# SP fetches the sixteenth gather of each step's last tile row by row, from row numbers loaded into registers

## What is computed

```
q = x @ Wq_pk;  sim = q . keys                 # per head, per side: 128 scores a token
scores, idx = top_k(sim, 16)                   # two sides
score = scores0[:, None] + scores1[None, :]    # 16 x 16 sums
final_scores, pk_idx = top_k(score, 16);  final_scores = softmax(final_scores)
ind = index[pk_idx] + head * 16384             # 16 rows of a table a token and head
k = sum_16 final_scores * keys_table[ind];  v = sum_16 final_scores * values_table[ind]
out = softmax(causal(q k^T)) v;  x = x + out @ Wo
```

## Time and profile before

| | |
|---|---|
| median of 3 runs | 10316.75 us (10314.2 to 10340.01) |
| the profiled execution, its own time | 10337.94 us |
| its span | 10336.0 us |
| busy: POOL, PE, DVE, ACT | 7772.2, 4872.7, 4777.3, 1478.0 us |
| granted PE clock, mean | 0.599 of full speed |

### The profile page before, as it was taken

One profiled execution on the slowest core, in us unless ns is written; L12 is line 12 of the kernel. 1 busy time (PEld: TensorE's weight loads), 2 busy tenths in 40 slices (PEclk: granted clock), 3 DMA queues, 4 the chain that ended last, 5 costly groups with the idle time before them and its releaser, 6 DMA issues.

```text
span 10336.0 us, 99229 instructions
## 1 busy us (share of the span) xinstructions
PE 4872.7 (47%) x26912; PEld 2864.2 (28%) x26912; DVE 4777.3 (46%) x21897; ACT 1478.0 (14%) x4051; POOL 7772.2 (75%) x8201
## 2 busy tenths in 40 slices
PE   4444444544445444444444444444444444444444
PEld 2222222322223222232222222222222222322222
DVE  5454444444444444444444444444454444444443
ACT  1111111111111111111111111111111111111111
POOL 6777777777777777777777777777777777777776
PEclk6565655656555565565655656556565565655655
DMA  3333333333333333333333333333333333333333
GB/s 106 105 111 105 105 111 105 111 105 105 111 105 111 105 105 112 105 111 105 105 111 105 112 105 105 111 105 111 105 105 111 105 111 105 105 111 105 106 105 97
DMA packets 420780, 1106.51 MB, mean 107 GB/s; under 512 B 131952, under 2 KB 149744, under 8 KB 420208
## 3 DMA queue, kind: packets, MB, share of 16 engines
q0 software_dynamic: 393216, 1074.27, 36.1%
q1 hardware_dynamic: 27120, 27.46, 0.9%
HBM read 1097.01 MB, written 4.19 MB: 107 GB/s over the span
## 4 chain that ended last, share of the span: by engine, by line
POOL 74%; issue 25%; PE 1%; POOLq 0%; DMA 0%; DVE 0%; ACT 0%; DVEq 0%
POOL got L242 74%; PE comb_ps L347 0%; DMA got<-in_table,rows 0%; POOLq L235 0%; POOLq L238 0%; POOLq L239 0%; POOLq L236 0%; PE front_ps L292 0%; POOLq L249 0%; PE front_ps L281 0%; PE score_ps L368 0%; PE score_ps L380 0%; DVE xn L584 0%; PE front_ps L272 0%; PE front_ps L311 0%
## 5 line engine op out<-in xcount | busy, mean ns | idle before, releaser
L242 POOL DMA_INDIRECT got<-in_table,rows x8192 | 7770.4, 949 | 2538.5 <-issue 2492.1
L347 PE MATMUL comb_ps<-got,spread 128*32 128x256 f32 x16384 | 1564.5, 548 | 3665.8 <-DMA got<-in_table,rows 3665.8
L347 PEld LDWEIGHTS comb_ps<-got,spread 128*32 128x32 f32 x16384 | 637.4, 150 | 4468.2 <-DMA got<-in_table,rows 3788.8
L725 DVE CUSTOM_DVE_ANT_0 neg<-score_ps,mask 128x128 f32<-128x128 f32 (+3 forms) x512 | 251.7, 492 | 2393.0 <-PE score_ps L368 2387.3
L745 DVE SCALAR_TENSOR_TENSOR acc<-probT_ps,prob_inv,acc 128x128 f32<-128x128 f32 x448 | 157.1, 351 | 1628.7 <-PE probT_ps L386 1628.7
L380 PE MATMUL score_ps<-probT,kv 128*128 128x128 f32 x2560 | 691.6, 433 | 269.6 <-ACT probT L426 269.6
L426 ACT ACTIVATE keyT<-probT_ps 128x128 f32<-128x128 f32 x512 | 142.1, 278 | 4198.5 <-PE probT_ps L358 4020.6
L368 PE MATMUL score_ps<-keyT,qT 128*128 128x128 f32 (+3 forms) x1024 | 578.9, 656 | 330.3 <-DVE spread L701 177.4
L374 PE MATMUL probT_ps<-ident,prob 128*128 128x128 f32 x1280 | 356.8, 397 | 754.8 <-ACT prob L502 754.8
L380 PEld LDWEIGHTS score_ps<-probT,kv 128*128 128x128 f32 x2560 | 550.5, 308 | 432.0 <-ACT probT L426 432.0
L374 PEld LDWEIGHTS probT_ps<-ident,prob 128*128 128x128 f32 x1280 | 194.8, 188 | 1138.7 <-ACT prob L502 1138.7
(11 more groups left out here) (99 smaller groups left out, 5640.1 us busy)
## 6 DMA issues: line engine op xcount, KB each, us to landing
got<-in_table,rows POOLq DMA_INDIRECT x8192, 2.7
adj_i<-in_adj SPq DMA_DIRECT2D x16, 1024.0 KB
x_in<-in_x SPq DMA_DIRECT2D x16, 256.0 KB, 3.5
out<-fin SPq DMA_DIRECT2D x16, 256.0 KB, 3.1
wqpk_sb<-in_wqpk_t SPq DMA_DIRECT2D x1, 512.0 KB, 10.6
keys_sb<-in_keys_t SPq DMA_DIRECT2D x1, 512.0 KB, 13.2
wq_sb<-in_wq SPq DMA_DIRECT2D x1, 512.0 KB, 13.4
wo_sb<-in_wo SPq DMA_DIRECT2D x1, 512.0 KB, 14.3
```

The source lines that it names most:

```text
L242: pool.indirect_dma_start(out=got[t][:, g, :], out_offset=None, in_=table, in_offset=bass.IndirectOffsetOnAxis(ap=rows[par][:, t * GATHERS ...
L347: mm = pe.matmul(comb_ps[t % 2][j * BAND:(j + 1) * BAND, 0:2 * D], spread[par][:, t, g, :], got[t][:, g, :], start=(c == 0), stop=(c == PE ...
```

## The change

The last of the 64 gathers of each step (tile 3, g = 15) is no longer issued by POOL. Instead:

- `move` for the pair that ends with tile 3 issues one more matmul, which puts the 128 row numbers of that gather side by side into one partition of PSUM (`last_ps`).
- `take_moved` adds the head's offset to them in one more DVE instruction, ahead of the others, into `rows_last[par]`, and counts up `last_ready`.
- SP, in the new function `fetch`, waits for `last_ready` and for the buffer, and then 16 times loads eight numbers into registers and issues eight DMAs, each of one table row of 1 KB into one partition of `got_last[par]`. All 128 count up `fetched[par]`. No run-time range check of the numbers is issued.
- PE's `combine(3)` waits for `fetched[par]` before its last matmul, and reads `got_last[par]` there.
- SP's loads and stores of the batches stand between these fetches.

```
+    got_last = [sb(f"got_last{i}", [P, 2 * D]) for i in range(2)]
+    rows_last = [sb(f"rows_last{i}", [1, P], U32) for i in range(2)]
...
+    last_ps = score_ps[0:1, 384:384 + P]
...
-        with sp.Fori(0, B - 1) as b:
+
+        def fetch(s, par, reuse=True):
+            sp.wait_ge(last_ready, s + 1)
+            sp.sem_inc(held, 1)
+            if reuse:
+                sp.wait_ge(combined, s * T - T)
+                sp.sem_inc(held, 1)
+            for p0 in range(0, P, 8):
+                _, row = nc.values_load_multi_w_load_instructions(
+                    rows_last[par][0:1, p0:p0 + 8], engines=[mybir.EngineType.SP], min_val=0, max_val=H * ROWS - 1,
+                    skip_runtime_bounds_check_because="a row number is a key of each side and a head")
+                for i in range(8):
+                    sp.dma_start(got_last[par][p0 + i:p0 + i + 1, :],
+                                 table[bass.ds(row[i], 1), :]).then_inc(fetched[par], 16)
+
+        def more(b):
+            with sp.Fori(0, H // 2 - 1) as i:
+                fetch(b * H + i * 2 + 2, 0)
+                fetch(b * H + i * 2 + 3, 1)
...
+        load_next(0)
+        fetch(0, 0, reuse=False)
+        fetch(1, 1, reuse=False)
+        more(0)
+        with sp.Fori(0, B - 2) as i:
+            load_next(i + 1)
+            fetch((i + 1) * H, 0)
+            store_last(i + 1)
+            fetch((i + 1) * H + 1, 1)
+            more(i + 1)
...
-                    for g in range(c, GATHERS, PER_BAND):
+                    for g in range(c, GATHERS - 1 if t == T - 1 else GATHERS, PER_BAND):
...
+            if t0 + nt == T:
+
+                mm = pe.matmul(last_ps, group_of[:, GATHERS - 1:GATHERS],
+                               lifted[:, nt - 1, 0, :, :].rearrange("p e r -> p (e r)"), start=True, stop=True)
...
+                        row_by_row = t == T - 1 and g == GATHERS - 1
+                        if row_by_row:
+                            pe.wait_ge(fetched[par], P * 16)
+                            pe.sem_clear(fetched[par])
                         mm = pe.matmul(comb_ps[t % 2][j * BAND:(j + 1) * BAND, 0:2 * D], spread[par][:, t, g, :],
-                                       got[t][:, g, :], start=(c == 0), stop=(c == PER_BAND - 1))
+                                       got_last[par][:, :] if row_by_row else got[t][:, g, :],
+                                       start=(c == 0), stop=(c == PER_BAND - 1))
...
+            if t0 + nt == T:
+                dve.tensor_scalar(rows_last[par][:, :], last_ps, head_row[0:1, bass.ds(h, 1)], None,
+                                  ALU.add).then_inc(last_ready, 1)
```

More of the change, by code:

```diff
@@ L154, in program @@
     gathered = [sem(f"gathered{t}") for t in range(T)]
+    fetched = [sem(f"fetched{i}") for i in range(2)]
+    last_ready = sem("last_ready")
     gathered_end = [sem(f"gathered_end{i}") for i in range(PER_BAND)]
@@ L207, in _, with load_next @@
         sp.sem_inc(fin_free, 1)
-        with sp.Fori(0, B - 1) as b:
+        def fetch(s, par, reuse=True):
[15 more added lines that the diff above has]
+                fetch(b * H + i * 2 + 3, 1)
+        def load_next(b):
             sp.wait_ge(x_used, b + 1)
@@ L212, in _, with store_last @@
             load_adj(b + 1)
-            sp.wait_ge(fin_ready, (b + 1) * T)
-            store(b)
-            sp.wait_ge(out_stored, (b + 1) * 16)
+        def store_last(b):
+            sp.wait_ge(fin_ready, b * T)
+            store(b - 1)
+            sp.wait_ge(out_stored, b * 16)
             sp.sem_inc(fin_free, 1)
+        load_next(0)
[8 more added lines that the diff above has]
+            more(i + 1)
+        fetch((B - 1) * H, 0)
+        store_last(B - 1)
+        fetch((B - 1) * H + 1, 1)
+        more(B - 1)
         sp.wait_ge(fin_ready, B * T)
@@ L337, in combine @@
                 end = last and t == T - 1
+                n = (GATHERS - 1 if t == T - 1 else GATHERS) * 16
                 if not end:
-                    pe.wait_ge(gathered[t], s * (GATHERS * 16) + GATHERS * 16)
+                    pe.wait_ge(gathered[t], s * n + n)
                 if t == 0:
@@ L343, in combine @@
                     if end:
-                        pe.wait_ge(gathered_end[c], BANDS * 16)
+                        pe.wait_ge(gathered_end[c], (BANDS - c // (PER_BAND - 1)) * 16)
                     for j in range(BANDS):
                         g = j * PER_BAND + c
+                        row_by_row = t == T - 1 and g == GATHERS - 1
+                        if row_by_row:
+                            pe.wait_ge(fetched[par], P * 16)
+                            pe.sem_clear(fetched[par])
                         mm = pe.matmul(comb_ps[t % 2][j * BAND:(j + 1) * BAND, 0:2 * D], spread[par][:, t, g, :],
-                                       got[t][:, g, :], start=(c == 0), stop=(c == PER_BAND - 1))
+                                       got_last[par][:, :] if row_by_row else got[t][:, g, :],
+                                       start=(c == 0), stop=(c == PER_BAND - 1))
                 mm.then_inc(combined, 1)
```

## The result

The changed kernel takes 10363.27 us (10357.43 to 10364.12), the kernel before 10317.0 (10314.2 to 10340.01): a ratio of 1.004, 95% interval 1.0024 to 1.0056. So it is slower, by 0.4%, not by 24%. The prediction's direction held, its size did not, and the time lies outside its range (11,250 to 14,400).

What follows compares the result with a forecast made beforehand. POOL's gathers bound the kernel at 80.2 us a step; SP's fetch of 87.4 us plus 11.9 would make a 99.3 us period, 127 of them 12611, with the ends 12,797, or 12,770 us as median. Range 11,250 to 14,400.

Steps and rivals of the forecast that it cites:

- Bound before, and what is won: POOL's 64 gathers set the pace at 80.2 us a step; removing one saves 1.25 us, 160 us over 128 steps.
- The loop: combine(3), tile 2's attention, move, SP's fetch, landing, next combine(3) run in series: a period of 99.3 us against POOL's 78.95.
- The rest of the loop: Everything in the period besides SP's fetch, from the landing through combine(3) to SP's start: 11.9 us a step.
- twice the same: From the end of combine(3) to rows, 9.1 us were read in two successive steps of the trace.
- the landing: From the end of SP's last issue until the row has landed: 2.0 us.
- The register loads: On SP, 16 loads of eight row numbers each fetch at 0.9 us, 14.4 us, with ends of 0.16 and 1.5 us.
- The pitch of a row: SP's time from one row's DMA to the next, register computation included: 0.57 us, 73.0 us for 128 rows.
- SP keeps up: Rival: with SP's fetch at most 67.0 us, POOL stays the bound and the kernel takes 10,157 us; chance 0.10.
- slower but under 11,250: Outcome of a slower kernel with a time below the forecast range; chance 0.04.
- Its sign of being wrong: The forecast fails if SP's pitch with loads is under 0.52 us, or a row's DMA takes longer than 0.45.
- The lower end for the pitch: Low estimate of SP's time per row, 0.46 us, from the pitch of two loads without register work.
- A little slower only: Rival: pitch 0.52 and loads 0.2 us give a fetch of 69.8 us and 10,540 us; slower under 11,250 got 0.04.

Runs made afterwards that it cites:

- early_move_b: Changed kernel, with the next step's row numbers for tiles 2 and 3 moved before combine(3) instead of after tile 2's attention; 10158.19 us, ratio 0.9846.
- mid_move_b: Changed kernel, with those row numbers moved directly after combine(3), ahead of tile 2's attention; 10157.43 us, ratio 0.9847 to the kernel before.
- half_rows_b: Changed kernel, with SP loading and fetching only 64 of the 128 rows, the other partitions staying zero; 10156.07 us, ratio 0.9846 to the kernel before.
- loads_of_16_c: Changed kernel, with eight register loads of 16 numbers in place of 16 loads of eight; 10160.02 us, ratio 0.9848 to the kernel before.
- double_loads_d: Changed kernel, with each group of eight numbers loaded twice into registers and both loads used; 11522.65 us, ratio 1.1171 to the kernel before.
- shapes: Changed kernel, with SP issuing DMAs of 1 to 128 rows and loads of 1 to 16 numbers before the first step; 18980.91 us beside 15569.
- first run, at 16440 us: Kernel before, with only the earlier move of the row numbers, run in the slow state; 16440 us beside 15577 for the kernel before.
- before_early: Kernel before, with only the earlier move of the row numbers and no fetch by SP; run again 10339.31 us against 10339.26, ratio 1.000.

## Why the prediction was wrong

**Bound before, and what is won.** Right: 1.25 us a step for the gather, 160 us in all, and 157 to 159 were measured in each of the four kernels whose loop lies under POOL's 79 us (`early_move_b`, `mid_move_b`, `half_rows_b`, `loads_of_16_c`).

**The loop.** Right, and shown from three sides: opened (`early_move_b`), lengthened (`double_loads_d`), shortened (`loads_of_16_c`).

**The rest of the loop**, predicted 11.9 us, measured 13.6. The last matmul was priced at 0.1 us, as a 32nd of a group in which they overlap; alone, after the wait, it takes 1.06. From there to `rows_last` 10.5 us passed (5043.45 to 5053.92), not 9.3. Two windows of the changed kernel, before and after the wait ends; behind the busy times of PE, PEld, DVE, ACT and POOL stand the granted clock, the share of the DMA engines and GB/s:

```profile
5026.00:5042.00 16.00, 0.00 (x0) 0.00 (x0) 2.88 (x5) 0.00 (x0) 12.04 (x14) 0.61 0.36 107
5042.40:5054.00 11.60, 8.73 (x27) 5.18 (x27) 1.16 (x5) 2.03 (x6) 8.84 (x10) 0.50 0.38 110
```

PE has stood idle for 16 us there and then does tile 2's attention at a granted clock of 0.50, the lower of its two levels, 1.2 GHz. The scores matmul of this place took 1.65 us (L422 at 5044.23), where the kernel before did it in 0.91 (L368 at 5023.20) in a stretch with a granted clock of 0.68. What the clock is worth stands in the trace of the kernel before. Two of its stretches from the end of `combine(3)` to `rows`, with the same work in them:

```profile
5263.42:5273.38 9.96, 7.09 (x23) 4.78 (x23) 1.09 (x5) 2.03 (x6) 7.52 (x9) 0.50 0.37 106
5022.58:5031.60 9.02, 6.15 (x23) 4.48 (x23) 1.08 (x4) 2.03 (x6) 6.89 (x8) 0.68 0.36 102
```

Of its 127 such stretches 32 were at 0.50 and took 9.96 us, 95 at 0.66 to 0.71 and took 9.0 on average. The prediction read two of the 95 and wrote "twice the same". In the changed kernel all 127 are at 0.50, so 0.9 us of the miss are the clock; the added matmul of `move`, 0.53 us in the chain where 0.2 were predicted, is the rest of the way to 10.5. That PE's longer wait (13.2 us a step on average) is what lowered the clock fits with this but is not shown: before, waits of 9.2 us stood ahead of a stretch at 0.68 and of one at 0.50. Against all this the landing was cheaper: from the end of the last issue to PE's start 1.3 us in the rows above and 1.4 on average, in place of 2.0. SP took 0.25 us from the end of `rows_last` to its first load, where 0.2 were estimated. The difference of 1.7 us is worth 212 us in all.

**The register loads**, predicted 16 x 0.9 = 14.4 us. Right, with the gap: 0.78 us and some 0.12 behind it, and 66.7 - 128 x 0.41 = 14.2. That it was so near is luck: no row showed such a load, and 0.9 was a choice between ends of 0.16 and 1.5.

**The pitch of a row: the step that failed.** The prediction asked "Is a DMA of one row cheaper to issue than one of 512?" and answered with 128 and 512 rows, which cost the same, so 0.57 us, 73.0 us in each step and by far the largest term of the sum. Measured: 0.41 (5040.06 to 5040.47 in the chain, one row after the other). The 0.15 us are the DMA's own, 225 ns in place of 373; computation and move were as read. `shapes` shows why the argument did not carry: from 16 rows up the price has no trend, and it falls only below that, so two points up there said nothing of the other end. 73.0 - 52.4 = 20.6 us a step, 2640 us in all. The path of the loop and the wait that ends last in it were as predicted; it was the size of this term that put the time outside the range. With both corrections the prediction's sum is 12,797 - 2640 + 212 = 10,369 for the profiled execution, which took 10364.12.

**That the sign held is luck.** With the fetch as measured, 66.7 us, and the rest as predicted, 11.9, the loop would have been 78.6 us, just under POOL's 78.95, and the kernel 1.5% faster. Only the second miss, 1.7 us too little in the rest of the loop, made it slower. The prediction itself had named this place: "0.41 with loads of 0.9" was where its rival *SP keeps up* was to begin, and pitch and loads came out just so. By its count the outcome, slower but under 11,250, had a chance of 0.04. Its sign of being wrong, a pitch with loads under 0.52 us, stood right at the edge: 66.7 / 128 = 0.52.

**The ends and the chances.** The lower end for the pitch, 0.46, was itself taken from 128-row loads, and the rival *A little slower only* (pitch 0.52) got 0.04. The text said that nothing showed what part of the 373 ns the rows were; the range should have taken that in, down to the register work and gaps alone (0.2 us), which would have put the low end at the other rival's 10,157. *SP keeps up* had the right rule, F at most POOL's 78.95 less the rest of the loop, and the wrong value: 67.0 by its sum, by which the changed kernel's 66.7 would have kept up, and 65.4 with the rest as measured. The changed kernel at 66.7 and `loads_of_16` at 63.6 stand on both sides of that.

**The two rules of the Trainium skill on loads.** "DMA: Bandwidth & Descriptors" ("Latency and other measured facts") has about 600 ns as the floor of a register load. Here 436 ns were measured with one number, and 527 with eight behind another load, so the floor is lower, and the measurements decide. As the whole price of a load of eight, the estimate that the prediction made of it, 0.6 us was too low: it took 0.78 us in the fetch, 0.9 with the gap. "Runtime: NRT & Kernel Launch" ("Instruction fetch mechanics") has about 200 ns a register. That page's register loads are from HBM; here the numbers lay in SBUF, and it was 56 ns a number above four, so the estimate of 1.6 us for eight was twice too high.

## What to carry to other kernels

When work moves from the engine that sets the pace to an idle one, look for the earliest moment at which its inputs exist and the moment at which its result is waited for. If both hang on the same event of successive steps, the new work forms a loop whose length is its own duration plus everything between. A second buffer doesn't shorten it: the changed kernel has one, and SP never waited for it. Such a loop cost nothing here while it was shorter than the old bound, and beyond it every microsecond counted whole: 3 us decided between 1.5% faster and 0.4% slower, and an earlier issue of the inputs, worth 0.0% by itself, took the question away. A duration should not be carried over from one shape to a much smaller one that no row shows, and a stretch with PE in it is best read over all its occurrences in a trace, since its clock may differ between them.

## What was unexpected of the hardware

- The price that SP pays to issue a DMA depends on its rows in a way that is not monotone: 252 ns for one, 420 for 16, 597 for 64, 432 for 128.
- A load of registers is dearer behind a DMA than behind another load: eight numbers took 0.78 us and 0.53 us. What the difference is was not tried.
- Each one-row DMA made two packets, not 16 pieces and more as the prediction allowed for: 59,888 on SP's queue against 27,120 in the kernel before, 32,768 more for 16,384 DMAs, one of 1 KB and one of 4 bytes for each.
- The same work of PE and its partners took 9.0 or 9.96 us in one trace, by the granted clock of the stretch (0.68 or 0.50).
- In its first run, at 16440 us, `before_early` had a wait of up to 64 us on ACT in each of the 128 steps, for something that the trace doesn't name. What it is stays open:

```profile
ACT keyT L430 <- remote: 8062.6, 128, 64.0
```
